# Expert gates stored beside the normed rows, a last norm in another order whose stores add to the residual

## The reference

```python
logits = einsum('bsh,eh->bse', h, gate_w) + expert_bias
weights = softmax(logits)
top_w, top_i = top_k(weights, 2)
top_w = top_w / (sum(top_w) + 1e-6)                 # two gates a token
for e in range(8):
    y = gelu(h @ w_up[e].T) @ w_down[e].T
    out = out + sparse_w[..., e:e+1] * y            # sparse_w holds top_w at top_i
out = (out - mean(out)) * rsqrt(var(out) + 1e-5)    # over the 256 features
ffn = out + h
x = x_after_attention + gb * ffn                    # gb: one row of 256 for each batch
```

## Time and profile before

| | |
|---|---|
| median of 3 runs | 1291.9 us (1290.64 to 1292.19) |
| the profiled execution, its own time | 1292.79 us |
| its span in the profile | 1291.0 us |
| PE busy | 1098.4 us (85%) |
| POOL busy | 858.3 us (66%) |
| DVE busy | 785.0 us (61%) |
| ACT busy | 641.2 us (50%) |

### The profile page before, as it was taken

How to read it: one execution, slowest core, us unless ns; L and a number is a source line. 1 busy time by engine, 2 the same in 40 slices (tenths; PEclk the granted TensorE clock), 3 DMA queues, 4 the chain that set the end, 5 groups by cost and what they waited for, 6 DMA issues and landing times. The chain is left out here.

```text
span 1291.0 us, 30710 instructions
## 1 busy us (share of the span) xinstructions
PE 1098.4 (85%) x11290; PEld 879.2 (68%) x11291; DVE 785.0 (61%) x2056; ACT 641.2 (50%) x913; POOL 858.3 (66%) x951
## 2 busy tenths in 40 slices
PE   5469999999999999999999503999999999999900
PEld 3237777777777777777777402888888888888800
DVE  4536667567685676856768276554555555455567
ACT  3438777776767767677677202222222222222222
POOL 2347588685976868768666428566666666767656
PEclk9779999999999999999999855999999999999955
DMA  8976753855548555485350380134424344342364
GB/s 293 275 207 188 206 166 77 205 140 112 168 100 204 134 110 162 114 196 136 90 161 11 114 299 24 39 81 83 110 45 110 48 111 114 74 85 45 45 162 134
DMA packets 122892, 167.14 MB, mean 129 GB/s; under 512 B 13048, under 2 KB 99320, under 8 KB 122784
## 3 DMA queue, kind: packets, MB, share of 16 engines
q1 hardware_dynamic: 103200, 137.59, 38.6%
q0 software_dynamic: 19584, 28.11, 11.9%
HBM read 105.22 MB, written 60.44 MB: 128 GB/s over the span
## 5 line engine op out<-in xcount | busy, mean ns | idle before, releaser
L932 DVE CUSTOM_DVE_ANT_0 b_sn<-b_ps_s,s_tile 128x512 f32<-128x512 f32 x512 | 341.3, 688 | 191.7 <-PE b_ps_s L1061 188.6
L874 ACT ACTIVATE b_pt<-b_ps_t 128x1024 f32<-128x1024 f32 x256 | 259.5, 1018 | 73.3 <-PE b_ps_t L1075 73.3
L1075 PE MATMUL b_ps_t<-s_ident,b_sn 128*128 128x128 f32 x2048 | 267.7, 273 | 3.0 <-POOL b_sn L774 1.2
L1075 PEld LDWEIGHTS b_ps_t<-s_ident,b_sn 128*128 128x128 f32 x2048 | 236.6, 141 | 40.7 <-issue 10.4
L1661 ACT ACTIVATE d_g<-d_ps_u 128x512 f32<-128x512 f32 x156 | 92.8, 598 | 314.9 <-PE d_ps_u L1774 308.3
L774 POOL TENSOR_SCALAR b_sn<-b_sn,b_mn 128x512 f32<-128x512 f32 x256 | 175.2, 695 | 101.2 <-DVE b_mn L932 100.8
L866 ACT ACTIVATE b_sn<-b_sn,b_mn 128x512 f32<-128x512 f32 x256 | 182.0, 722 | 92.4 <-DVE b_mn L932 85.4
L1061 PE MATMUL b_ps_s<-s_ks,s_qs 96*128 96x512 bf16 x512 | 179.1, 386 | 28.1 <-PEq L144 18.0
L1774 PE MATMUL d_ps_u<-d_xp,k_wu 128*128 128x256 bf16 x1776 | 201.8, 274 | 0.0
L1789 PE MATMUL d_ps_y<-k_wd,d_gp 128*128 128x256 bf16 x1776 | 199.9, 273 | 0.0
L1774 PEld LDWEIGHTS d_ps_u<-d_xp,k_wu 128*128 128x128 bf16 x1776 | 173.7, 98 | 21.6
(11 more groups left out here) (199 smaller groups left out, 1191.5 us busy)
## 6 DMA issues: line engine op xcount, KB each, us to landing
w_parts<-b_w_split SPq DMA_DIRECT2D x32, 512.0 KB, 3.6
splits<-s_parts SPq DMA_DIRECT2D x32, 384.0 KB, 2.9
s_qs<-splits SPq DMA_DIRECT2D x96, 128.0 KB, 5.9
s_ks<-splits SPq DMA_DIRECT2D x96, 128.0 KB, 7.4
b_w_raw<-in_w_up_t SPq DMA_DIRECT2D x16, 512.0 KB, 10.8
b_w_raw<-in_w_down_t SPq DMA_DIRECT2D x16, 512.0 KB, 7.1
k_wu<-w_parts SPq DMA_DIRECT2D x8, 1024.0 KB
k_wd<-w_parts SPq DMA_DIRECT2D x8, 1024.0 KB
```

The lines of the kernel that those rows point to most:

```text
L874: act.activation(pt[:, m, 2 * pair:2 * pair + 2, :], ps_t[:, 2 * pair:2 * pair + 2, :], ACT.Exp).then_inc(exped, 1)
L932: dve.tensor_tensor_reduce(sn[:, n % 2, t, :], ps_s[:, t % 2, :], ahead.tile[:, n, at:at + S], -1.0, BIG, ALU.add, ALU.min, mn[:, n % 2, t ...
L1075: mm = pe.transpose(ps_t[:, j, t * P:(t + 1) * P], sn[:, m, t, j * P:(j + 1) * P], ident[:, :])
```

## The change

The two gates of a token are stored as two more columns of its row in `h2_rows`, whose rows grow from 256 to 258 numbers (`GW`). The gather of the rows brings them along. Which of the two belongs to a place is in a new table of ones and zeros (`kept.choice`), and DVE multiplies and adds in each step (`choose_gates`). The gathers of the gates, `gate_rows`, `rest_rows` and `kept.rest` are gone: `attention` stores the rest straight to `out`, and the stores of the last norm add to it in DRAM; they are issued by POOL, not SP. ACT scales all rows of the last norm, and DVE and POOL add nothing any more. DVE's order in the last norm is another. The empty steps stay behind the filled ones, as before.

```diff
+GW = D + 2
...
-        self.rest = sb("rest", [P, NT, D])
...
-        self.gates = sb("gates", [P, 2, NT])
+        self.gates = sb("gates", [P, NT, 2])
...
-        self.places = sb("places", [P, TABLE, 2, TT], U32)
+        self.places = sb("places", [P, TABLE, TT], U32)
+        self.choice = sb("choice", [P, TABLE, TT, 2])
...
-            sp.dma_start(gate_rows.rearrange("(p i) a -> p (i a)", p=P), kept.gates[:, :, :].rearrange("p k t -> p (k t)")).then_inc(gates_out, 16)
-            sp.dma_start(kept.rest[:, :, :], rest_rows.rearrange("b (t p) d -> p (b t) d", p=P)).then_inc(kept_in, 16)
+            sp.dma_start(h2_rows.rearrange("(t p) d -> p t d", p=P)[:, :, D:GW], kept.gates[:, :, :],
+                         allow_slow_non_contiguous=True).then_inc(gates_out, 16)
...
             def load(t, u):
 
                 at_least(pool, turned, t - 1)
+                apart(pool, pool_passed)
+                at_least(pool, gates_chosen, t - 1)
                 apart(pool, pool_passed)
...
-                for i in range(TT):
-                    pool.indirect_dma_start(gates[:, u, i:i + 1], None, gate_rows,
-                                            bass.IndirectOffsetOnAxis(ap=places[:, u, 1, i:i + 1], axis=0)).then_inc(gates_in[u], 16)
...
-            def deviations(b):
+            def deviations(b, end):
...
-            def finish(b):
-
-                at = slice(b * TB + BY_DVE, (b + 1) * TB)
-                pool.wait_ge(normal, (b + 1) * (TB - BY_DVE))
-                pool.tensor_tensor(y[:, at, :], y[:, at, :], kept.rest[:, at, :], ALU.add).then_inc(done_pool, 1)
-
-            for b in range(0, B, 2):
-                deviations(b)
-                for k in range(b, b + 2):
-                    finish(k)
+            def add_to_rest(b):
+
+
+                pool.wait_ge(normal, (b + 1) * TB)
+                pool.dma_start(out[b, :, :].rearrange("(t p) d -> p t d", p=P), y[:, b * TB:(b + 1) * TB, :],
+                               accum_op=ALU.add).then_inc(stored, 16)
+
+            deviations(0, 1)
+            deviations(1, 2)
+            for k in range(2):
+                add_to_rest(k)
+            deviations(2, 4)
+            for k in range(2, 4):
+                add_to_rest(k)
+            deviations(4, 6)
+            deviations(6, 8)
+            for k in range(4, B):
+                add_to_rest(k)
...
-                act.wait_ge(gates_in[u], (t - u) * 16 + 32)
+                act.wait_ge(gates_ready, t + 1)
...
+            def choose_gates(t, u):
+
+                dve.wait_ge(x_in[u], (t - u) * 16 + 32)
+
+                at_least(dve, y_ready, (t - 1) * TT)
+                dve.tensor_tensor(both_gates[:, u, :, :], xg[:, u, :, D:GW],
+                                  kept.choice[:, bass.ds(t, 1), :, :].rearrange("p a i k -> p (a i) k"), ALU.mult).then_inc(gates_chosen, 1)
+                dve.wait_ge(gates_chosen, t + 1)
+                dve.tensor_tensor(gates[:, u, :], both_gates[:, u, :, 0], both_gates[:, u, :, 1], ALU.add).then_inc(gates_ready, 1)
+
             def step(t, u):
                 if not is_last(t):
                     split_x(t + 1, 1 - u)
+                    choose_gates(t + 1, 1 - u)
...
-            for b in range(2):
-                moments(b)
-            for b in range(0, B, 2):
-                for k in range(b, b + 2):
-                    centre(k)
-                for k in range(b + 2, min(b + 4, B)):
-                    moments(k)
-                for k in range(b, b + 2):
-                    finish(k)
+            for b in (0, 1):
+                moments(b)
+            for b in (0, 1):
+                centre(b)
+            for b in (2, 3):
+                moments(b)
+            for b in (2, 3):
+                centre(b)
+            for b in (4, 5, 6, 7):
+                moments(b)
+            for b in (4, 5, 6, 7):
+                centre(b)
```

More of the change, by code:

```diff
@@ L497, with attention @@
 FROM_BEFORE = ("back3", "turn0", "turn1", "out0", "out1", "rows0", "rows1", "logits")
-def attention(nc, ahead, logits, x, h1t, mod_rows, ext_rows, splits, w_up_t, w_down_t, w_parts, rest_rows, h2_rows, sums):
+def attention(nc, ahead, logits, x, h1t, mod_rows, ext_rows, splits, w_up_t, w_down_t, w_parts, out, h2_rows, sums):
     GROUPS = NH // TB
@@ L1241, in __init__, with route @@
         self.wd = sb("wd", [P, 2, PIECES, NIC, D], BF16)
-def route(nc, kept, logits, rest_rows, mod_rows, expert_bias, w_parts, gate_rows):
+def route(nc, kept, logits, mod_rows, expert_bias, w_parts, h2_rows):
     FILLS = TABLE * TT
@@ L1391, in _ @@
             for k in range(2):
[L1392 removed]
+                dve.tensor_tensor(kept.gates[:, :, k], top[:, :, k], per_tok[:, 3, :], ALU.mult).then_inc(gates_set, 1)
             link(dve.tensor_copy(top_f[:, :, :], top_i[:, :, 0:2]))
@@ L1473, in _ @@
             link(ins)
[L1474 to L1477, removed]
+            dve.tensor_scalar(kept.places[:, :, :], by_tile[:, 2, :, :], -1.0, None, ALU.add)
+            dve.tensor_scalar(kept.choice[:, :, :, 1], by_tile[:, 0, :, :], float(B * S), None, ALU.is_gt)
+            link(dve.tensor_scalar(source[:, 3, :], source[:, 0, :], 0.0, None, ALU.is_gt))
+            dve.tensor_tensor(kept.choice[:, :, :, 0], by_tile[:, 3, :, :], kept.choice[:, :, :, 1], ALU.subtract)
         @block.tensor
@@ L1494, in _, with experts @@
             mm.then_inc(tokens_found, 1)
-def experts(nc, kept, w_parts, h2_rows, gate_rows, sums, out):
+def experts(nc, kept, w_parts, h2_rows, sums, out):
     BANKS = 4
+    FROM = (0, 1, 2, 4, 6)
     with ExitStack() as ctx:
@@ L1572, in _ @@
                              ).then_inc(y_in[b], 16)
-            for b in range(B):
-                sp.wait_ge(done_dve, (b + 1) * BY_DVE)
-                sp.wait_ge(done_pool, b + 1)
-                sp.dma_start(out[b, :, :].rearrange("(t p) d -> p t d", p=P), y[:, b * TB:(b + 1) * TB, :]).then_inc(stored, 16)
-            sp.wait_ge(stored, 16 * B)
         @block.gpsimd
@@ L1683, in scale @@
             def scale(b):
-                act.wait_ge(rstd_done, b // 2 + 1)
-                for t in range(b * TB + BY_DVE, (b + 1) * TB):
+                act.wait_ge(rstd_done, sum(1 for k in FROM if k <= b))
+                for t in range(b * TB, (b + 1) * TB):
                     act.wait_ge(centred, t + 1)
@@ L1715, in _ @@
             split_x(0, 0)
+            choose_gates(0, 0)
             by_tiles(dve, step)
@@ L1732, in centre @@
                                              op0=ALU.subtract, op1=ALU.mult).then_inc(centred, 1)
-            def finish(b):
-                dve.wait_ge(rstd_done, b // 2 + 1)
-                dve.wait_ge(centred, (b + 1) * TB)
-                for t in range(b * TB, b * TB + BY_DVE):
-                    dve.scalar_tensor_tensor(out=y[:, t, :], in0=y[:, t, :], scalar=rstd[:, t:t + 1], in1=kept.rest[:, t, :],
-                                             op0=ALU.mult, op1=ALU.add).then_inc(done_dve, 1)
-            for b in range(2):
-                moments(b)
-            for b in range(0, B, 2):
-                for k in range(b, b + 2):
-                    centre(k)
-                for k in range(b + 2, min(b + 4, B)):
-                    moments(k)
-                for k in range(b, b + 2):
-                    finish(k)
+            for b in (0, 1):
+                moments(b)
+            for b in (0, 1):
[8 more added lines that the diff above has]
+                centre(b)
         @block.tensor
@@ L1836, in adaln_block @@
             attention(nc, ahead, logits, x, h1t, mod_rows, ext_rows, splits,
-                      w_up_t, w_down_t, w_parts, rest_rows, h2_rows, sums)
+                      w_up_t, w_down_t, w_parts, out, h2_rows, sums)
         kept = Kept(nc, ctx)
-        route(nc, kept, logits, rest_rows, mod_rows, expert_bias, w_parts, gate_rows)
-        experts(nc, kept, w_parts, h2_rows, gate_rows, sums, out)
+        route(nc, kept, logits, mod_rows, expert_bias, w_parts, h2_rows)
+        experts(nc, kept, w_parts, h2_rows, sums, out)
 def kernel(**inputs):
```

43 lines of the change are left out of this document (20 added, 23 removed).

## The result

| | before | after |
|---|---|---|
| median | 1292.05 us (4 runs, 1290.64 to 1295.33) | 1313.72 us (4 runs, 1313.38 to 1314.51) |
| profiled execution: span | 1291.0 us | 1312.3 us |
| first `up` to the end of the last product | 417.9 | 444.3 |
| from there to the end | 63.9 | 61.3 |
| ahead of the first `up` | 809.3 | 806.8 |

A forecast was written before the change was run, and what follows sets the result against it. PE was taken to bound the steps without a gap, with the last norm behind it. Steps +28.1, tail -7 and `route` -0.2 gave +21 us, so 1312 us; 80% for 1300 to 1323.

The forecast's parts named there:

- +28.1 for the steps: Steps with a tile before them: 36 delays of PE at a mean of 0.78 us; bounds +22 and +34.
- -7 behind them: After the last product: earlier POOL, new norm and adding stores end 7 us sooner; between -15 and +3.
- DVE's new wait: In each step, `choose_gates` waits for ACT's result ahead of bank 0, so `down` loads weights 0.82 or 0.74 us late.
- the term of 0.78 a step: Mean delay of the weight loads of `down`, charged to PE in each of 36 steps.
- banks 1 to 3 add nothing: In `down`: these banks follow at most 1.2 us apart and PE takes 1.31 per quarter, so no further delay.
- The last norm: After the last product: DVE no longer waits for POOL, first store issued at 1254.5, ACT done near 1272.
- `route`: Ahead of the steps: the rest's load goes, the gates' small stores stay hidden under 40 us of cover; 0.2 us saved.
- the bound of 67: In `route`: upper limit of 67 us for storing the gates as 4096 pieces of 8 bytes.
- Rival 1: Whole kernel faster: PE's delay under 0.5 us a step, adding stores at 48 ns; 1289 us with 0.45 a step; 5%.
- Rival 2: The tail gives nothing: adding stores at 127 ns or empty scatters landing as before; 1320 to 1323 us; 10%.
- Rival 3: In `route`: the gates' store outlasts its cover, ending 27 us late at the 67 us bound; 1339 us; 3%.
- Rival 4: In the steps: PE's clock falls because of short idles, 1.7 us a step; 1375 us; 2%.

The follow-up runs named there:

- late choice: The changed kernel with `choose_gates` behind the four banks instead of ahead of them, its wait kept; 1291.19 us, 0.9982 of before.
- Gates in a table: The changed kernel with chosen gates kept in a buffer with a place for every step, so DVE needs no wait for ACT's result; 1291.10 us, 0.9983 of before.
- deviations early: SP waits, with POOL also computing the deviations of the next two batches before issuing the stores of these two; 1285.23 us, 0.9952 of before.
- SP waits: late choice with SP instead of POOL waiting for the landing of the last stores; 1290.28 us, 0.9979 of before.
- norm only: The kernel before, its gate gathers kept, with the new last norm and its stores that add; 1296.55 us, 1.0028 of before.
- gates only: The changed kernel with the last norm of before: rest in SBUF, DVE and POOL adding it, SP storing; 1309.44 us, 1.0123 of before.
- late choice and old norm: gates only with `choose_gates` moved behind the four banks; 1287.55 us, 0.9953 of before.
- centring ahead: late choice and old norm, with DVE taking moments of and centring batches 2 and 3 ahead of the first finish; 1282.37 us, 0.9926 of before.

## Why the prediction was right, and where it was not

**The sign and the size.** 1312 us was forecast and 1313.7 measured. Both large terms were too far from zero: +28.1 for the steps, where the profiles differ by 26.4, and -7 behind them, where it is 2.6. They sum to +23.8 instead of +21, and the 2.5 us by which this profile happened to be shorter ahead of the steps bring it back to +21.3. So part of the exactness of the total is luck. Some of the working was loose without bearing on the argument: the load of the rest at 48 ns a KB is 12.3 us and not 12.6; the 127 ns are a mean over 288 packets of which 32 carry 4 bytes, and the 256 rows alone took 140 on average and 102 in the median; 1312.8 was given as 1312, and the lower end, 1292 + 22 - 12, as 1300.

**DVE's new wait** did what the steps said: ACT's result, then two small operations, then bank 0, then PE. I put the weights of `down` 5.96 us behind `up` in one kind of step (1222.66 less 1216.70) and 5.87 in the other (1210.97 less 1205.10); `down` began at 6.01 and 5.81. What was mis-sized is the term of 0.78 a step: I counted how much later the weights are loaded. PE loses less, as its loads had run ahead of the products by 0.10 us (1221.84 against 1221.94 in the timeline of before). The products are 0.67 later, and 36 of these are 24.1. Over all tiles of the two traces, from the start of `up` to that of `down`, it is 24.4 from the second tile on. Of the other 2.0 us the first `up` is 0.5 (7.54 us to the start of `down` instead of 7.03), which is no effect of the wait: in late choice it was 7.73. The last 1.5 lie between `down` and the next `up`, 0.04 a step; what makes them isn't shown. A step grew from 11.32 to 12.03 us, where I had said 12.1 to 12.3. That banks 1 to 3 add nothing held: behind the first bank PE doesn't idle in `down`. Gates in a table showed that the wait is what makes the loss, as the operations were left in place.

**The last norm.** The early part was read right: sums loaded 9.1 us behind the last product (9.0 forecast), deviations begun at 24.2 (23.8). Behind that the term of -7 was mis-sized. The tail was to be 56.8 us and is 61.3: its first packet is 1.9 us later than forecast, the stream as long as forecast, and the end 2.7 us longer.

First, the stream of adding stores. I took 102 ns for a packet of 1 KB and no gap, 26 us. The DMA view of the changed kernel from 1297 to 1307 (queue, packets, MB, share of 16 engines) has:

```profile
q0 software_dynamic: 1893, 1.89, 122.4%
```

1.224 x 10 x 16 / 1893 is 103 ns for a packet, just as taken. But a share above 100% says that an engine has more than one packet in hand: it passes one every 10 x 16 / 1893 = 84.5 ns. With 8 small packets to 256 rows an engine passes 264, 22.3 us at that rate and not 26. The stream without gaps of deviations early, in which the rate was not held throughout, took 23.6, from 1256.4 to 1280.1. Here it still took 26.6, from 1281.7 to 1308.3, and so it did in SP waits (26.6), because of the gaps that I had said would not be there: ACT waited 3.99 and 3.68 us for deviations that POOL computes only behind the stores, each of which holds it for 1.3 to 1.4 us. The two errors, of some 2.5 us for the price and 3 for the gaps, cancel: luck again. The first store was issued 28.7 us behind the last product, not 27.3, and its packets came 2.0 us behind that, not 1.5.

Second, the end. I took 1.3 us for the landing and the end, as behind SP's stores. From the last packet of POOL's it was 4.0, of which POOL's drain is 3.17, and 3.0 in the experiment in which SP waited. This is the largest miss of the term: I had carried the price of an end behind SP's stores over to one behind POOL's.

The experiments with one half each show what the two parts of the term are: POOL's removed gathers give 6.6 us, and the new norm costs 4.0 to 4.4 of them. The step that failed is the claim that adding stores behind a quicker DVE and ACT would end sooner than the old norm.

**`route`.** Hidden as said. The 4096 pieces of 8 bytes were moved in the 3.4 us from 757 to 760.4, by the DMA view of the changed kernel:

```profile
q1 hardware_dynamic: 4118, 0.04, 62.7%
```

That is a duration of 0.627 x 3.4 x 16 / 4118 = 8.3 ns for each, one in 3.4 x 16 / 4118 = 13.2 ns on an engine, and 3.4 us for all of them, against the bound of 67. The Trainium skill (DMA: Bandwidth & Descriptors, the table at its head) says that transfers under 512 B are read-modify-write, which would speak for a high price of such a store; this one shows none that its cover of 40 us could feel.

**The rivals.** Rival 1 (faster) fell at the wait, 0.71 a step and over its 0.5, and at its stores, which took 84.5 ns and not 48. Rival 2 (the tail gives nothing) came near: 2.6 us are left, by another mechanism than the 127 ns that it named. Rival 3 is the row above. Rival 4, the clock, is settled by a window over 310 of the 444 us of the steps (columns as in the earlier trace rows):

```profile
925.00:1235.00 310.00, 291.67 (x2589) 249.84 (x2588) 156.21 (x310) 80.66 (x156) 157.99 (x156) 1.00 0.37 78
```

The window shows PE 94% busy over 310 us, with 0.57 to 0.77 lost ahead of every `down`, and the granted clock stayed at 1.00, the 2.4 GHz level. It was 1.00 from 815 to 925 and from 1235 to 1251 as well, and below it only in the first `up` (0.70 from 806 to 815), as it had been before the change. The kernel in which short idles made the clock swing, of which the Trainium skill tells (TensorE: Matmul & The Clock Gate, psum-queue depth-cycling), is not this one.

**What stays open.** Of the 4 us that the new norm costs, 2.5 came back with the gaps closed and SP waiting. The remaining 1.6 (58.4 against 56.8) aren't the stream's length, since the last packet then moves 0.6 us earlier than with the old norm: they are the time behind the last packet, 3.0 us against 0.7, which POOL's drain sets. It is not known what the drain waits for; its end came 2.7 to 3.8 us behind the last packet in the kernels in which POOL had issued the stores (3.8 after the change, 3.0 in norm only, 2.7 in SP waits).

## What to carry to other kernels

Look at what is queued behind a new wait, not at what the waiting instruction costs: two operations of 0.16 us, put with their wait ahead of the work that PE needs next, cost 26 us in the steps, and 1.2 and 0.4 when they stood behind it or had a buffer of their own. When a change has two halves, time each alone: here one half's gain behind the last product hid that the other was a loss. And when a rate is worked out from the DMA share, divide packets by time too: above 100% an engine has several packets in hand, and the duration of one is more than what it costs. Last, when a stretch has no busy engine and no transfer, ask for the instructions that the sum of busy time leaves out: here it was a drain of 3 us.

## What the runs showed of the hardware

- Stores that add in DRAM, issued in rows of 1 KB, flow at 84.5 ns for a packet and engine in a stretch of 10 us of the changed kernel (190 GB/s over 16), 1.8 times the 48 ns of plain ones, with a duration of 103 ns each; over a whole stream of 4.2 MB without gaps it was 180 GB/s (deviations early).
- The issue of such a store of 512 KB holds POOL for 1.3 to 1.4 us.
- From the last packet of POOL's stores to the end of the span it is 4.0 us when POOL waits for them (3.2 in norm only) and 3.0 when SP does. Behind SP's own plain stores it is 0.7 (gates only, late choice and old norm, centring ahead), and 1.5 in the kernel before. The difference is POOL's drain at the end of the program: 3.17 us in the changed kernel, 2.43 in norm only, begun when all its stores had landed; where SP waited it ran beside the stores for 12.18 and 14.30 us and ended 2.7 us behind their last packet.
- Pieces of 8 bytes to DRAM last 8.3 ns each and pass at one in 13.2 ns on a DMA engine, when 4096 of them go in one transfer (changed kernel).
